# Memory attention in fours of heads: scores in row halves, one score buffer, one group ahead

## The chip, the core and the metric

The kernel runs on one core of one Trainium2 chip. The metric is the time of one execution in microseconds on the device; lower is better. The program is one long kernel with six stages that run one after the other. The change touches the second of them.

## What is computed

The input x has 64 sequences of 128 tokens with 128 features. Six layers are applied, each added to x: causal attention, memory attention, a mixture of experts, an attention with SiLU, an attention over a context, and a feed-forward layer with 4-bit rounding. The stage in question is memory attention (the reference passes it a layer norm of x, and it norms once more by itself):

```python
xn = layernorm(x)                         # over 128 features, x being normed already
q = split_heads(xn @ Wq)                  # 16 heads of 64
k, v = split_heads(xn @ Wkv)
mem = split_heads(memories @ Wm)          # 77 tokens of context
k = concatenate([k, mem]); v = concatenate([v, mem])    # 128 + 77 = 205 keys
attn = softmax(q @ k.T * 64 ** -0.5)
return (attn @ v) @ Wo + bo
```

## The kernel before

Everything is in float32 and x stays in SBUF. `stage_memory_attention` (line 563) writes out by hand, for each engine, the order of its instructions, and joins the engines by semaphores; `over_sequences` (line 75) runs each engine's `step` for the 64 sequences, in pairs of an even and an odd one (p is the parity, which selects the buffer). An engine's queue is in order: an instruction behind a waiting one waits too.

A step has eight groups of two heads (i = 0 to 7). For each group the tensor engine (PE) makes the scores of two heads (`score`, line 671, 128 x 410 in one PSUM bank; two banks `sc` alternate, so scores run two groups ahead). Each head's q stands in a zero-padded 128-row buffer `qx`, so that a matmul over all 128 rows against the two heads' keys gives one head's scores. The vector engine (DVE) takes the minimum of the negated scores (`lowest`, line 755), the scalar engine (ACT) takes exponentials and their sums (`exponentials`, line 895, an activation of 205 columns for each head), DVE divides (`divide`, line 763: a reciprocal and two multiplications), PE transposes (`transposes`, line 685, four 128 x 128 blocks), and the transposed probabilities are copied from PSUM to SBUF (`copy_probs`), by DVE for even i (line 777) and by ACT for odd i (line 906). PE multiplies with the values (`values`, line 697, two heads in column halves of the array).

Between these, in the same queues, stands the work of the next sequence: PE projects q, k, v and the context's values in chunks of 512 columns (`project`, line 645; kinds "q", "k", "v", "mv"), and for every second sequence the context's keys ("mk", four chunks of 308 columns for the pair); ACT copies each chunk out (`copy_projection`, line 863). Two PSUM banks `pj` alternate: chunk k waits until chunk k - 2 is copied (line 649). `CHUNKS` and `SLOT` (lines 615 to 619) say which chunk goes with which group. `project_out` (line 712) makes the output of the sequence before and DVE adds it to x with the bias (`residual`, line 792). Two layer norms stand on DVE (lines 801 to 824), with their reciprocal roots on POOL (`norm_rsqrt`, line 132). The SP queue loads the context for each pair of sequences (line 628).

PE's order in a step, which the change rewrites, is:

```python
for i in range(NP):
    score(b, p, i + 2)          # or of sequence b + 1
    transposes(b, i)
    ...                         # transpose_x, projections of b + 1
    values(b, p, i - 1)         # or of sequence b - 1
    if i == 2 and not first:
        project_out(b - 1)
```

Of the kernel before, what the change touches and what calls it, by code (L numbers as in the profile page):

```python
# [562 lines left out]
def stage_memory_attention(nc, X, w, consts, tiles):  # L563
# [5 lines left out]


    KN = S + CK
    with ExitStack() as ctx:
# [6 lines left out]
        qx = mem.sbuf("qx", [128, 2, XH, 128])  # L579
# [3 lines left out]
        low = mem.sbuf("low", [128, 2, 2])  # L583
        sums = mem.sbuf("sums", [128, 2, 2])
        rec = mem.sbuf("rec", [128, 2, 2])
        pr = mem.sbuf("pr", [128, 2, 2, 256])
        pn = mem.sbuf("pn", [128, 2, 2, 256])
        prT = mem.sbuf("prT", [128, 2, 2, 2, 128])
        oT = mem.sbuf("oT", [128, NP, 128])
# [4 lines left out]
        po = mem.psum("po", [128, 512])  # L594
        pm = mem.psum("pm", [128, 512])
        p_xT, p_y = pm[:, 0:128], pm[:, 128:256]
# [7 lines left out]
        tr_made = mem.sem("tr_made")  # L604
        prT_even, prT_odd = mem.sem("prT_even"), mem.sem("prT_odd")
        pv_made, oT_made = mem.sem("pv_made"), mem.sem("oT_made")
        y_made, y_added, x_written = mem.sem("y_made"), mem.sem("y_added"), mem.sem("x_written")
        ln = NormBuffers(mem, "ln")
        ln2 = NormBuffers(mem, "ln2")

        CHUNKS = [[("mk", 0), ("mk", 1), ("mk", 2), ("mk", 3), ("q", 0), ("k", 0), ("q", 1), ("k", 1), ("v", 0),
                   ("v", 1), ("mv", 0), ("mv", 1)],
                  [("mv", 0), ("mv", 1), ("q", 0), ("k", 0), ("q", 1), ("k", 1), ("v", 0), ("v", 1)]]
        SLOT = [[[0, 1], [2, 3], [4], [5], [6], [7, 8], [9, 10], [11]],
                [[0], [1], [2], [3], [4], [5], [6], [7]]]
# [5 lines left out]
        with nc.Block() as block:  # L625
            @block.sync
            def _(sp):
                def load(j):
                    if due(20 * j - 6):
                        sp.wait_ge(pj_made, 20 * j - 6)  # L630
                    sp.dma_start(cT[:], w["ctxT"].rearrange("(j r) d k -> j d r k", r=2)[j]).then_inc(c_loaded, 16)

                load(0)
                with sp.Fori(1, B // 2) as j:
                    load(j)

            @block.tensor
            def _(pe):
                def transpose_x(b, p):
                    pe.wait_ge(ln2.xn_done, b + 1)  # L640
                    if due(b - 2):
                        pe.wait_ge(y_added, b - 2)
                    pe.transpose(p_xT, ln2.xn[:, p], consts.ident[:]).then_inc(xT_made, 1)

                def project(b, p, k):
# [25 lines left out]
                def score(b, p, i):  # L671
                    n = NP * b + i
                    if due(n - 1):
                        pe.wait_ge(exped, n - 1)
                    if i == 0:
                        pe.wait_ge(ck_moved, b + 1)
                        pe.wait_ge(pj_copied, chunks(b, p) + CHUNKS[p].index(("k", 0)) + 1)
                    if i == 4:
                        pe.wait_ge(pj_copied, chunks(b, p) + CHUNKS[p].index(("k", 1)) + 1)
                    for h in range(2):  # L680
                        last = pe.matmul(sc[:, i % 2, KN * h:KN * h + KN], qx[:, p, 2 * i + h], kT[:, p, i],  # L681
                                         start=True, stop=True)
                    last.then_inc(scored, 1)

                def transposes(b, i):
                    n = NP * b + i
                    pe.wait_ge(normed, 2 * n + 2)
                    if due(NP // 2 * b + i // 2):
                        pe.wait_ge(prT_odd if i % 2 else prT_even, NP // 2 * b + i // 2)
                    for h in range(2):  # L690
                        for t in range(2):
                            o = 256 * h + 128 * t
                            last = pe.transpose(tr[:, i % 2, o:o + 128], pn[:, i % 2, h, 128 * t:128 * t + 128],  # L693
# [3 lines left out]
                def values(b, p, i):  # L697
                    pe.wait_ge(prT_odd if i % 2 else prT_even, NP // 2 * b + i // 2 + 1)
                    if i == 0:
                        pe.wait_ge(pj_copied, chunks(b, p) + len(CHUNKS[p]))  # L700
                    if i % 4 == 0:
                        if due(2 * b + i // 4):
                            pe.wait_ge(oT_made, 2 * b + i // 4)
                    for t, v in enumerate((vt, vm)):
                        for h in range(2):
                            f = XD * (2 * i + h)
                            last = pe.matmul(po[XD * h:XD * h + XD, 128 * (i % 4):128 * (i % 4) + 128],  # L707
                                             v[:, p, f:f + XD], prT[:, i % 2, h, t], start=t == 0, stop=t == 1,
                                             tile_position=(0, XD * h))
                    last.then_inc(pv_made, 1)  # L710

                def project_out(b):
                    pe.wait_ge(oT_made, 2 * b + 2)
                    if due(b):
                        pe.wait_ge(y_added, b)

                    pe.wait_ge(xT_copied, b + 3 if not isinstance(b, int) else min(b + 3, B))
                    for i in range(NP):
                        last = pe.matmul(p_y, oT[:, i], wo[:, i], start=i == 0, stop=i == NP - 1)
                    last.then_inc(y_made, 1)  # L720

                def step(b, p, last):
                    first = isinstance(b, int) and b == 0
                    for i in range(NP):
                        if i < NP - 2:
                            score(b, p, i + 2)
                        elif not last:
                            score(b + 1, 1 - p, i + 2 - NP)
                        transposes(b, i)
                        if i == 0 and not last:  # L730
                            transpose_x(b + 1, 1 - p)
                        if not last:
                            for k in SLOT[1 - p][i]:
                                project(b + 1, 1 - p, k)
                        if i > 0:
                            values(b, p, i - 1)
                        elif not first:
                            values(b - 1, 1 - p, NP - 1)
                        if i == 2 and not first:
                            project_out(b - 1)  # L740
                    if last:
                        values(b, p, NP - 1)
                        project_out(b)

                pe.wait_ge(zeroed, 4)
# [4 lines left out]
                score(0, 0, 1)  # L750
# [3 lines left out]
            def _(dve):  # L754
                def lowest(b, i):
                    n = NP * b + i
                    if due(n - 1):
                        dve.wait_ge(exped, n - 1)
                    dve.wait_ge(scored, n + 1)
                    dve.tensor_reduce(low[:, i % 2], sc[:, i % 2, 0:2 * KN].rearrange("p (h k) -> p h k", h=2),  # L760
                                      AX.X, ALU.min).then_inc(low_found, 1)

                def divide(b, i):

                    n = NP * b + i
                    if due(2 * n - 2):
                        dve.wait_ge(normed, 2 * n - 2)
                    dve.wait_ge(exped, n + 1)
                    dve.reciprocal(rec[:, i % 2], sums[:, i % 2]).then_inc(rec_made, 1)  # L769
                    if due(n - 1):  # L770
                        dve.wait_ge(tr_made, n - 1)
# [1818 lines left out]
```

## Time and profile before

| | before |
|---|---|
| median of 3 runs | 4079.44 us (4078.22 to 4080.56) |
| span of the profiled execution | 4078.1 us |
| that execution's own time, apart from its span | not given; the three runs lie within 2.5 us of the span |
| PE busy over the span | 3652.5 us (90%) |
| DVE, ACT, POOL busy | 63%, 62%, 41% |
| PE clock over the span, mean granted | 0.939 of full |
| first instruction of memory attention | 641.99 us (the first memset) |
| last output projection of the stage, last matmul begins | 2283.3 us |

Times are microseconds from the span's start. A row of a timeline gives the start, the time from start to the last one's end, and the operation; since an engine overlaps neighbouring instructions, the cost of an instruction in its queue is the distance from its start to the next one's start (its slot), which is shorter than its duration. A float32 matmul shows as two records. The bracket at the end is the idle time before, and who ended it. PEclk is the clock that PE was granted, 1.00 being 2.4 GHz and 0.50 being 1.2 GHz.

### The profile page before, as it was taken

Reading aid. Unit: us, or ns where it says so; the run is one execution under the profiler, and the core shown is the slowest. Engines: PE = TensorE matmul, PEld = TensorE weight load, DVE = VectorE, ACT = ScalarE, POOL = GpSimd, SP = SyncE. Lnnn points to the kernel's source line nnn. Section 1 sums busy time; section 2 is a strip of 40 time slices with the busy share of each in tenths; the row PEclk is TensorE's granted clock in tenths of the full one; section 3 lists DMA queues with packets and bytes.
Section 4 is the critical chain, followed back from the end, with each engine's and each line's share of the span. In section 5 each row is a group of like instructions: output and inputs, shape, how many; then the busy total and the mean of one; then the engine's idle time right before and its main releaser. Section 6 shows DMA issues by size and latency. Waiting matters only on the chain. (4 is left out here: it accounts for less than half of the span.)

```text
span 4078.1 us, 99545 instructions
## 1 busy us (share of the span) xinstructions
PE 3652.5 (90%) x26897; PEld 2556.5 (63%) x26989; DVE 2573.4 (63%) x8223; ACT 2526.2 (62%) x9209; POOL 1690.9 (41%) x2468
## 2 busy tenths in 40 slices
PE   8999998999999999999999614879999799995776
PEld 5565666777777777777777513654444466663444
DVE  7888885555555555555555520126666688887997
ACT  6888886666666666666666201235555699993221
POOL 6888882000000000000000142038888577774665
PEclk9999999999999999999999657989999899997776
DMA  4000000000000000000000102210000000000000
GB/s 119 0 0 0 0 0 3 2 2 2 2 2 2 2 2 2 2 2 2 2 2 1 63 26 64 81 44 9 9 9 9 5 6 5 5 5 3 13 10 16
DMA packets 80213, 53.87 MB, mean 13 GB/s; under 512 B 24785, under 2 KB 74397, under 8 KB 80016
## 3 DMA queue, kind: packets, MB, share of 16 engines
q1 hardware_dynamic: 76048, 44.89, 3.9%
q0 software_dynamic: 4096, 8.16, 0.7%
q8 instruction: 31, 0.51, 0.1%
q14 instruction: 38, 0.31, 0.0%
HBM read 32.29 MB, written 20.97 MB: 13 GB/s over the span
## 5 line engine op out<-in xcount | busy, mean ns | idle before, releaser
L135 POOL TENSOR_TENSOR b_ln_var_eps<-b_ln_mean_var,all_eps 128x1 f32<-128x1 f32 x128 | 33.3, 260 | 1476.8 <-DVE b_ln_mean_var L129 1476.8
L681 PE MATMUL b_sc<-b_kT,b_qx 128*128 128x205 f32 x2048 | 485.2, 360 | 1.2 <-ACT b_pr L901 1.2
L901 ACT ACTIVATE b_pr<-b_sc,b_low 128x205 f32<-128x205 f32 x1024 | 431.8, 429 | 68.6 <-DVE b_low L760 64.0
L467 ACT ACTIVATE a_pr<-a_sc,a_low 128x128 f32<-128x128 f32 x1024 | 365.4, 383 | 37.1 <-POOL a_pn L511 26.5
L782 DVE COPY b_prT<-b_tr 128x512 f32<-128x512 f32 x256 | 177.1, 692 | 322.4 <-PE b_tr L693 322.4
L681 PEld LDWEIGHTS b_sc<-b_kT,b_qx 128*128 128x128 f32 x2048 | 330.4, 189 | 78.9 <-issue 77.1
L774 DVE TENSOR_SCALAR b_pn<-b_pr,b_rec 128x205 f32<-128x205 f32 x1024 | 289.4, 325 | 58.8 <-DVE b_rec L769 7.4
L2090 ACT ACTIVATE f_pr<-f_sc,f_low 128x77 f32<-128x77 f32 x1024 | 320.2, 338 | 10.2 <-DVE f_low L1981 2.9
L693 PE MATMUL b_tr<-all_ident,b_pn 128*128 128x128 f32 x2048 | 307.7, 273 | 2.7 <-DVE b_pn L774 2.4
L760 DVE TENSOR_REDUCE b_low<-b_sc 128x2 f32<-128x410 f32 x512 | 295.4, 577 | 19.2 <-PE b_sc L681 19.1
L502 POOL TENSOR_TENSOR a_kx<-a_qk,w_hsel 128x512 f32<-128x512 f32 x256 | 292.1, 1152 | 2.4 <-DVE a_qk L338 2.4
L1488 PE MATMUL d_sc<-d_qx,d_qk 128*128 128x512 f32 x512 | 288.4, 646 | 0.0
L254 PE MATMUL a_sc<-a_kx,a_qk 128*128 128x512 f32 x512 | 262.7, 595 | 11.7 <-POOL a_kx L502 9.2
L769 DVE RECIPROCAL b_rec<-b_sums 128x2 f32<-128x2 f32 x512 | 82.1, 160 | 300.5 <-ACT b_pr L901 300.3
L693 PEld LDWEIGHTS b_tr<-all_ident,b_pn 128*128 128x128 f32 x2048 | 255.1, 140 | 20.8 <-DVE b_pn L774 4.2
L881 ACT ACTIVATE b_qx<-b_pj 64x512 f32<-64x512 f32 x256 | 151.5, 592 | 150.7 <-PE b_pj L658 149.2
L707 PEld LDWEIGHTS b_po<-b_prT,b_vt 128*64 128x64 f32 x2048 | 101.4, 135 | 210.5 <-issue 183.5
L1592 ACT ACTIVATE d_at<-d_sc 128x512 f32<-128x512 f32 x256 | 152.9, 597 | 125.6 <-PE d_po L1498 124.7
L467 ACT ACTIVATION_READ_ACCUMULATOR a_pr<-a_sc,a_low 128x1 f32 x1024 | 227.4, 222 | 0.0
L911 ACT ACTIVATE b_prT<-b_tr 128x512 f32<-128x512 f32 x256 | 153.2, 598 | 119.3 <-PE b_tr L693 119.3
L707 PE MATMUL b_po<-b_prT,b_vt 128*64 128x128 f32 x2048 | 225.4, 298 | 0.0
L2090 ACT ACTIVATION_READ_ACCUMULATOR f_pr<-f_sc,f_low 128x1 f32 x1024 | 223.6, 218 | 0.0
(278 smaller groups left out, 9605.9 us busy)
## 6 DMA issues: line engine op xcount, KB each, us to landing
scratch_x<-r_zeros SPq DMA_DIRECT2D x12, 512.0 KB, 5.0
e_xr<-scratch_x SPq DMA_DIRECT2D x24, 256.0 KB, 3.1
scratch_y<-e_yr SPq DMA_DIRECT2D x24, 256.0 KB, 2.4
all_X<-in_x SPq DMA_DIRECT2D x8, 512.0 KB, 6.8
e_w<-in_e_w SPq DMA_DIRECT2D x16, 256.0 KB, 3.1
out_x<-all_X SPq DMA_DIRECT2D x8, 512.0 KB, 3.2
w_mask<-in_mask SPq DMA_DIRECT2D x1, 2464.0 KB, 10.6
b_cT<-in_ctxT SPq DMA_DIRECT2D x32, 77.0 KB, 1.9
```

Of the source, the lines that this page charges most:

```text
L254: pe.matmul(sc[:, u % 2], qk[:, p, 0], kx[:, p, u], start=False, stop=True).then_inc(scored, 1)
L467: op = act.activation(pr[:, u % 2, g], sc[:, u % 2, 128 * g:128 * g + 128], ACT.Exp, bias=low[:, u % 2, g:g + 1], scale=-1.0, accum_out=su ...
L502: pool.tensor_tensor(kx[:, p, u], qk[:, p, 1].unsqueeze(1).broadcast_to([128, NG, 128]), hsel[:, NG * u:NG * u + NG].unsqueeze(2).broadcas ...
L681: last = pe.matmul(sc[:, i % 2, KN * h:KN * h + KN], qx[:, p, 2 * i + h], kT[:, p, i], start=True, stop=True)
L693: last = pe.transpose(tr[:, i % 2, o:o + 128], pn[:, i % 2, h, 128 * t:128 * t + 128], consts.ident[:])
L707: last = pe.matmul(po[XD * h:XD * h + XD, 128 * (i % 4):128 * (i % 4) + 128], v[:, p, f:f + XD], prT[:, i % 2, h, t], start=t == 0, stop=t ...
L760: dve.tensor_reduce(low[:, i % 2], sc[:, i % 2, 0:2 * KN].rearrange("p (h k) -> p h k", h=2), AX.X, ALU.min).then_inc(low_found, 1)
L774: dve.tensor_scalar(pn[:, i % 2, h, 0:KN], pr[:, i % 2, h, 0:KN], rec[:, i % 2, h:h + 1], None, ALU.mult).then_inc(normed, 1)
L782: dve.tensor_copy(prT[:, i % 2].rearrange("p h t q -> p (h t q)"), tr[:, i % 2])\
L901: op = act.activation(pr[:, i % 2, h, 0:KN], sc[:, i % 2, KN * h:KN * h + KN], ACT.Exp, bias=low[:, i % 2, h:h + 1], scale=-1.0, accum_out ...
L1488: pe.matmul(sc[:, u % 2], qk[:, p, 1], qx[:, p, u], start=True, stop=True).then_inc(scored, 1)
L2090: op = act.activation(pr[:, u % 2, g], sc[:, u % 2, CK * g:CK * g + CK], ACT.Exp, bias=low[:, u % 2, g:g + 1], scale=-1.0, accum_out=sums[ ...
```

## The change

- **Groups.** A step has four groups of four heads (j = 0 to 3), each in two halves (i = 0, 1) of two heads.
- **Scores.** The padded `qx` becomes a dense `q`. A head's scores come from a matmul over 64 rows (`tile_position=(64 * h, 0)`), rows 0 to 63 for h = 0 and 64 to 127 for h = 1, each h into a bank of its own. The two banks now hold one group, so there is one score buffer, and scores run one group ahead. One `lowest` covers four heads (820 columns).
- **Transposed probabilities.** All `copy_probs` are on DVE. `prT` keeps two buffers, now the halves of one group. The values of a group come in one go at the end of the group, for the group itself.
- **Order.** On PE, DVE and ACT it is written anew, see the diff. Chunks go in lists `EARLY` (between the two halves' transposes) and `LATE` (after the second).
- **mv.** The context's values are no longer a matmul of 512 columns but four transposes of the context's keys.
- **PSUM.** `po`, `p_xT` and `p_y` share a bank; `po` holds one group and is copied by four `copy_out` of 256 columns instead of two of 512; `oT` gets two buffers.
- **Norms.** The two layer norms are made in one pass: the second's statistics and application on DVE go, and POOL works out the product of both roots in seven small operations (`both_norms`). The bias is added on POOL (`add_bias`).
- **Start.** The memsets of `qx` and `pr` go. The wait of the context's load is on an earlier chunk, as its buffer is read by mk alone.

The core of the diff (semaphore counts that only follow the new numbering left out):

```diff
-        qx = mem.sbuf("qx", [128, 2, XH, 128])
+        q = mem.sbuf("q", [128, 2, NP, 128])
...
+        EARLY = [[[0, 1, 2, 3], [], [6], [9]], [[], [], [2], [5]]]
+        LATE = [[[4], [5], [7, 8], [10, 11]], [[0], [1], [3, 4], [6, 7]]]
...
-                        half = wm[:].rearrange("p (c i) d -> p c (i d)", c=2)[:, c]
-                        last = pe.matmul(dst[0:CK], cT[:, p], half, start=True, stop=True)
+                        for t in range(4):
+                            last = pe.transpose(dst[0:CK, 128 * t:128 * t + 128], ck[:, 4 * c + t, p], consts.ident[:])
...
+                def score(b, p, j):
+                    n = NJ * b + j
+                    if due(2 * n):
+                        pe.wait_ge(exped, 2 * n)
...
+                    for i in range(2):
+                        for h in range(2):
+                            r = slice(XD * h, XD * h + XD)
+                            last = pe.matmul(sc[:, h, KN * i:KN * i + KN], q[r, p, 2 * j + i],
+                                             kT[r, p, 2 * j + i], start=True, stop=True, tile_position=(XD * h, 0))
                     last.then_inc(scored, 1)
...
+                def values(b, p, j, last_sequence):
+                    n = NJ * b + j
+                    pe.wait_ge(prT_made, 2 * n + 2)
...
             @block.tensor
...
                 def step(b, p, last):
+                    for j in range(NJ):
+                        if j < NJ - 1:
+                            score(b, p, j + 1)
                         elif not last:
+                            score(b + 1, 1 - p, 0)
+                        transposes(b, j, 0)
+                        if j == 0 and not last:
+                            transpose_x(b + 1, 1 - p)
+                        if j == 1 and not first:
+                            project_out(b - 1, 1 - p, NJ * b + 1)
                         if not last:
+                            for k in EARLY[1 - p][j]:
                                 project(b + 1, 1 - p, k)
+                        transposes(b, j, 1)
+                        if not last:
+                            for k in LATE[1 - p][j]:
+                                project(b + 1, 1 - p, k)
+                        values(b, p, j, last)
...
             @block.vector
...
                 def step(b, p, last):
+                    for j in range(NJ):
+                        copy_probs(b, j, 0)
+                        if j == 0 and ahead:
                             norm_statistics(dve, ln, X[:, b + 2], b + 2, p)
...
+                        if more:
+                            lowest(nb, nj)
+                        if j == 0 and ahead:
+                            norm_moments(dve, ln, p)
+                        if more:
+                            divide(nb, nj, 0)
+                        if j == 1 and not (isinstance(b, int) and b == 0):
+                            residual(b - 1)
+                        copy_probs(b, j, 1)
+                        if j == 1 and not last:
+                            move_context_keys(b + 1, 1 - p)
+                        if j == 2 and ahead:
+                            dve.wait_ge(xT_made, b + 1)
                             norm_apply(dve, ln, X[:, b + 2], b + 2, p)
+                        if more:
+                            divide(nb, nj, 1)
...
             @block.scalar
...
                 def step(b, p, last):
+                    for j in range(NJ):
+                        if j > 0:
+                            copy_out(b, p, j - 1)
...
+                        if more:
+                            exponentials(nb, nj, 0)
+                        if j == 0 and not last:
                             copy_xT(b + 1, 1 - p)
+                        if more:
+                            exponentials(nb, nj, 1)
+                            for k in EARLY[1 - p][j]:
                                 copy_projection(b + 1, 1 - p, k)
+                        if not last:
+                            for k in LATE[1 - p][j]:
+                                copy_projection(b + 1, 1 - p, k)
```

(nb, nj) is the next group: (b, j + 1), or (b + 1, 0) after the last of a sequence.

## Rows read from the trace of the kernel before

**Rows 1.** The windows view of the steady part: busy us and instructions by engine, PEclk, DMA

```profile
702.63:2236.00 1533.37, 1533.37 (x11699) 1215.83 (x11697) 866.51 (x2727) 1050.92 (x3093) 98.43 (x242) 1.00 0.01 2
```

**Rows 2.** The instructions of line 719: ns min/median/max, first and last start

```profile
L719 PE MATMUL b_pm<-w_wo,b_oT x1024: 275/275/582, 699.8 to 2283.3; 128*128 128x128 f32 x171
```

**Rows 3.** PE timeline near the stage's end: start us, us, line, operation, count, idle before

```profile
2242.38 2.05 PE L719 MATMUL b_pm<-w_wo,b_oT 128*128 128x128 f32 x16
...
2276.39 0.73 PE L693 MATMUL b_tr<-all_ident,b_pn 128*128 128x128 f32 x4 [1.22 <-DVE b_pn L774]
2277.05 0.70 PE L707 MATMUL b_po<-b_prT,b_vt 128*64 128x128 f32 x4
```

**Rows 4.** PE timeline of one sequence in the steady part, same columns

```profile
1200.83 1.21 PE L662 MATMUL b_pj<-b_cT,w_wm 128*128 128x154 f32 x8
...
1205.37 2.05 PE L719 MATMUL b_pm<-w_wo,b_oT 128*128 128x128 f32 x16
1207.26 0.86 PE L681 MATMUL b_sc<-b_kT,b_qx 128*128 128x205 f32 x4
...
1209.38 0.44 PE L707 MATMUL b_po<-b_prT,b_vt 128*64 128x128 f32 x4
...
1209.97 0.96 PE L681 MATMUL b_sc<-b_kT,b_qx 128*128 128x205 f32 x4
1210.76 0.60 PE L693 MATMUL b_tr<-all_ident,b_pn 128*128 128x128 f32 x4
1211.20 1.06 PE L658 MATMUL b_pj<-b_xT,w_wq 128*128 128x128 f32 x8
1212.19 0.44 PE L707 MATMUL b_po<-b_prT,b_vt 128*64 128x128 f32 x4
```

**Rows 5.** ACT timeline of the same stretch

```profile
1200.21 0.43 ACT L901 ACTIVATE b_pr<-b_sc,b_low 128x205 f32<-128x205 f32 x1
...
1201.09 0.60 ACT L911 ACTIVATE b_prT<-b_tr 128x512 f32<-128x512 f32 x1
1201.59 0.92 ACT L887 ACTIVATE b_ck<-b_pj 128x308 f32<-128x308 f32 x2
...
1224.40 0.46 ACT L860 ACTIVATE b_xT<-b_pm,w_gain 128x128 f32<-128x128 f32 x1 [0.59 <-PE b_pm L643]
```

**Rows 6.** DVE timeline of the same stretch

```profile
1199.87 0.28 DVE L123 BATCH_NORM_STATS2 b_ln_stats<-all_X 128x6 f32 x1
1201.24 0.17 DVE L769 RECIPROCAL b_rec<-b_sums 128x2 f32<-128x2 f32 x1 [1.09 <-ACT b_pr L901]
1201.52 0.57 DVE L774 TENSOR_SCALAR b_pn<-b_pr,b_rec 128x205 f32<-128x205 f32 x2
1202.00 0.58 DVE L760 TENSOR_REDUCE b_low<-b_sc 128x2 f32<-128x410 f32 x1
...
1204.07 0.69 DVE L782 COPY b_prT<-b_tr 128x512 f32<-128x512 f32 x1 [1.40 <-PE b_tr L693]
1204.68 0.15 DVE L769 RECIPROCAL b_rec<-b_sums 128x2 f32<-128x2 f32 x1
...
1208.16 0.58 DVE L760 TENSOR_REDUCE b_low<-b_sc 128x2 f32<-128x410 f32 x1 [0.17 <-PE b_sc L681]
1208.66 0.28 DVE L794 TENSOR_TENSOR all_X<-b_pm,all_X 128x128 f32 x1
```

**Rows 7.** Groups of DVE reductions: count, busy us, mean ns, idle before

```profile
L760 DVE TENSOR_REDUCE b_low<-b_sc 128x2 f32<-128x410 f32 x512 | 295.4, 577 | 19.2 <-PE b_sc L681 19.1
...
L1137 DVE TENSOR_REDUCE r_top<-r_logits 128x64 f32<-128x512 f32 x1 | 0.7, 686 | 0.0
```

**Rows 8.** DVE timeline of the stage's start

```profile
641.99 3.47 DVE L833 MEMSET b_qx<- 128x4096 f32 x1 [2.51 <-PEq L89]
```

**Rows 9.** The windows view of this stage's end and the last stage, as Rows 1

```profile
2270.00:2280.00 10.00, 6.75 (x57) 4.42 (x53) 4.44 (x13) 4.15 (x12) 0.00 (x0) 0.84 0.00 1
...
3800.00:3900.00 100.00, 74.67 (x254) 47.63 (x255) 94.57 (x354) 22.31 (x72) 65.83 (x112) 0.70 0.04 11
```

More of the change, by code:

```diff
@@ L700, in values @@
                         pe.wait_ge(pj_copied, chunks(b, p) + len(CHUNKS[p]))
[L701 to L709, printed above, removed]
@@ L710, in values @@
-                    last.then_inc(pv_made, 1)
[L712 to L717, printed above, removed]
+                        if not last_sequence:
+                            pe.wait_ge(xT_copied, b + 2)
+                    if j == 1 and due(b):
+                        pe.wait_ge(y_added, b)
@@ new lines, in values @@
+                    if due(n):
+                        pe.wait_ge(oT_made, n)
+                    for i in range(2):
+                        for t, v in enumerate((vt, vm)):
+                            for h in range(2):
+                                f = XD * (4 * j + 2 * i + h)
+                                last = pe.matmul(po[XD * h:XD * h + XD, 128 * i:128 * i + 128], v[:, p, f:f + XD],
+                                                 prT[:, i, h, t], start=t == 0, stop=t == 1,
+                                                 tile_position=(0, XD * h))
@@ L718, in project_out @@
+                    last.then_inc(pv_made, 1)
+                def project_out(b, p, free):
+                    pe.wait_ge(oT_made, free)
                     for i in range(NP):
-                        last = pe.matmul(p_y, oT[:, i], wo[:, i], start=i == 0, stop=i == NP - 1)
+                        last = pe.matmul(p_y, oT[:, p, i], wo[:, i], start=i == 0, stop=i == NP - 1)
                     last.then_inc(y_made, 1)
@@ L825, in step @@
-                        if i == 3 and not (isinstance(b, int) and b == 0):
-                            residual(b - 1)
-                        if i == 4 and not last:
-                            move_context_keys(b + 1, 1 - p)
+                        more = j < NJ - 1 or not last
+                        nb, nj = (b, j + 1) if j < NJ - 1 else (b + 1, 0)
+                        if more:
+                            lowest(nb, nj)
+                        if j == 0 and ahead:
+                            norm_moments(dve, ln, p)
@@ L920, in copy_out @@
                                    ACT.Copy).then_inc(oT_made, 1)
                 def step(b, p, last):
[L923 to L934 removed]
+                    for j in range(NJ):
+                        if j > 0:
+                            copy_out(b, p, j - 1)
+                        elif not (isinstance(b, int) and b == 0):
+                            copy_out(b - 1, 1 - p, NJ - 1)
+                        more = j < NJ - 1 or not last
+                        nb, nj = (b, j + 1) if j < NJ - 1 else (b + 1, 0)
+                        if more:
+                            exponentials(nb, nj, 0)
+                        if j == 0 and not last:
```

282 lines of the change are left out of this document (115 added, 167 removed).

## Prediction

> **What bounds the kernel now.** I read the windows view first. Over 1533 us of memory attention PE is busy for 1533.37 us at PEclk 1.00, while DVE is busy for 867 us and ACT for 1051 us [rows 1]: PE alone sets this stage's time. Its period follows from the output projections, one for a sequence: the first begins at 699.8 us for sequence 0 [rows 2], that of sequence 61 at 2242.38 us [rows 3], so a sequence takes 1542.6 / 61 = 25.29 us.
>
> The PE timeline gives the slots, from one start to the next [rows 4]: scores of two heads 0.79 (1209.97 to 1210.76), four transposes 0.44, a chunk of q or k 0.99, the values of two heads 0.59 (1209.38 to 1209.97), the output projection 1.89, and two mk chunks 1.21, so 0.6 each. For v and mv chunks, also 512 columns, I take 0.99. A sequence is 8 x 0.79 + 8 x 0.44 + 4 x 0.99 + 4 x 0.99 + 8 x 0.59 + 1.89 + 1.2 (mk, mean of even and odd) + 0.1 = 25.7, near the 25.29 measured. The slots can be trusted to 2%.
>
> **PE's work after.** If the two row halves run together, the scores of four heads take the slot of two: 4 x 0.79 saved, 3.2 us. The mv chunks become four transposes each: 2 x (0.99 - 0.44) = 1.1 us saved. That leaves 25.3 - 4.3 = 21.0 us a sequence. If PE stayed the bound this would be the new period.
>
> **The loop that the new order closes.** With one score buffer and the values of group n ahead of the scores of group n + 2 on PE, I follow one group from its scores and count what each step waits for:
> - PE: scores of n + 1, slot 0.79, then the transposes of n's first half, 0.60 to their end [rows 4]: 1.39. The scores end earlier (0.96).
> - DVE begins 0.04 after PE's end: scores end at 1207.26 + 0.86 = 1208.12 [rows 4], the reduction begins at 1208.16 [rows 6]. I use 0.04 for every hand-over. The copy of the probabilities stands first in DVE's queue: slot 0.61 (1204.07 to 1204.68) [rows 6]. Total 2.04.
> - The minimum over 820 columns: 577 ns for 410 and 686 ns for 512 make 1.07 ns a column [rows 7], so 0.577 + 410 x 1.07 ns = 1.02, an estimate. 3.06.
> - Hand-over 0.04, then ACT's two exponentials until DVE's reciprocal: 1200.21 [rows 5] to 1201.24 [rows 6], 1.03. 4.13.
> - Reciprocal 0.28, two multiplications 0.48 (1201.24, 1201.52, 1202.00) [rows 6]. 4.89.
> - Only now the copy of the second half, behind the division in DVE's queue: 0.69, and 0.04. 5.62.
> - PE, waiting for it, makes the values of four heads: 2 x 0.59 = 1.18. 6.80. The next scores stand behind them.
>
> So 6.80 us a group or 27.2 a sequence, with no engine full: more than the 25.29 of today. On top:
> - j = 0 has the norm's statistics (0.28 [rows 6]) between the first copy and the minimum, j = 1 the residual (0.28) ahead of the second copy: +0.56.
> - j = 2 and 3 have a third chunk (mv) whose bank comes free by a copy that ACT makes behind both pairs of exponentials: start at 3.10, two pairs at 0.88 (1200.21 to 1201.09 [rows 5]), the copy 0.60, hand-over 0.04, gives 5.50, the transposes 0.44, gives 5.94 against 5.62: +0.32 each, +0.64.
> - j = 0 ahead of an even sequence has four mk chunks between the two transposes, and the third waits for ACT's copy of the first, behind four exponentials and the copy of xT. ACT begins at 3.38, +0.88, xT +0.46, +0.88, copy of a chunk 0.46 (0.92 for two) [rows 5] and 0.04: 6.10; two mk chunks 1.2 [rows 4]: 7.30; transposes 0.60, hand-over, copy 0.69, hand-over: 8.67 against 5.90. +2.77, each second sequence: +1.4.
>
> Together 27.2 + 0.56 + 0.64 + 1.4 = 29.8 us, 4.5 more than today, and 63 periods give +284 us.
>
> **What costs or gives nothing.** ACT loses four copies of probabilities and two of four q copies, DVE gains the four copies and loses a norm's pass: both have room beside a 29 us period [rows 1]. POOL gets seven small operations and the bias; it is busy for 98 of 1533 us [rows 1], and the norm is used two groups later. The four smaller `copy_out` run in ACT's idle time ahead of the minimum. SP's load waits for an earlier chunk, so comes sooner. The output projection (1.89) and the other chunks lie in PE's wait for the second copy (from 1.4 to 5.6 us of a group). If the loop were shorter than 21.0 / 4 = 5.3 us, these would show. At the start the memset of qx goes (3.47 [rows 8]) and one pass of the norm: about 5 us less.
>
> Sum without the clock: 4078 + 284 - 5 = 4357 us, by the profiled span of 4078.1; the median is 1.3 us above it, too little to carry.
>
> **The row halves.** No row shows them. The nearest is column halves: four value matmuls of 128 columns take 0.59, four full ones of a q chunk 0.99 [rows 4], so two halves do overlap, if not wholly. Bounds for a group's scores: 0.4 (half the slot that I take; four heads without any weight-load time between) and 1.58 (no overlap). I take 0.79, two full slots of one head each. The Trainium skill's "TensorEngine Tiling (Array Packing)", section Tiling Modes, says that tiles work independently, which would give 0.79 as well, but also that changing the tiling mode drains the engine, which speaks against this change, as scores now are a mode of their own. The rows bound that: values to scores, a column mode and then a full one, take 0.59, and wholly overlapped halves without a drain would take 0.99 / 2 = 0.50, so a switch costs at most 0.09. Two more switches in a group would make the sum 0.18 x 4 x 64 = 46 us longer; I leave this to the range.
>
> **The clock.** PE now idles. In the first group of a sequence it has nothing from 1.8 us (both transposes) until q, which needs xT at 4.76. The trace shows what such gaps do: at the stage's end, with waits of 1.22 us, the transposes stretch from 0.60 to 0.73 and the values from 0.44 to 0.70 [rows 3], and the granted clock is 0.84 [rows 9], part of it at 1.2 GHz. At 1.2 GHz the loop's PE parts, 0.79 + 0.44 + 1.18, grow by 2.4 us. Bounds: nothing, or one such group in each sequence, 2.4 x 64 = 154 us. I take the middle, +77. Forecast 4357 + 77 = 4434.
>
> **Rivals.**
> - *Row halves in turn.* Scores 1.58 at the head of the loop: +0.79 x 4 x 64 = +202, 4640 us. For it: no row. Against: the column halves. Here the change would not do what it says.
> - *Low clock throughout.* The last stage, PE busy 75%, is granted 0.70 [rows 9], more than half of its time at 1.2 GHz. At 0.75, half the time, each group loses 1.2 us: +5 us a sequence on 4357, about 4670. Against: PE here works 21.0 of 29.8 us in bursts of full speed. The skill's "TensorE: Matmul & The Clock Gate", section "Why this matters for your kernels", names idle gaps between bursts as what takes the clock down; by it this rival gains.
> - *Short scores.* 0.4 instead of 0.79 and no clock loss: 4357 - 100 = 4257.
> - *PE stays the bound, faster.* Should the second copy not wait for the division, that is, should the loop of a group be under 5.3 us, the period is 21.0: 4078 - 4.3 x 63 - 5 = 3802. It turns faster than today already when the loop falls under (25.29 - 2.6) / 4 = 5.7 us. The place is DVE's queue between minimum and second copy. Against: the order is written out, and 1.03 + 0.28 + 0.48 are measured; the sum would need to be 1.1 us wrong.
>
> **How the numbers follow.** Forecast case 0.62, own range 4357 to 4520; row halves in turn 0.15; low clock throughout 0.10; short scores 0.08; PE-bound or a loop under 5.7, 0.03; within 0.2% of today 0.02 (0.2%, 8 us, is what a measurement of this kernel can tell). The range 4290 to 4650 holds the forecast, the row halves in turn and half of the short scores; most of the low clock and the faster case are left out. Faster 0.03, same 0.02, slower 0.95. The likeliest case gives 4434.
>
> **What would show it.** The PE timeline should have gaps ended by DVE's copy (`b_prT`) ahead of the values, in every group; PE busy near 75% in this stage; a distance of about 6.8 us from scores to scores, 7 for j = 0 and near 9.6 ahead of even sequences; the reduction at 1.0 us; PEclk under 1.00 around j = 0. Wrong it would be if PE were busy throughout, if scores of four heads took 1.6 us, or if DVE's second copy began before the division ended.

## The result and the profile after

The changed kernel takes 4523.88 us in the median of 4 runs (4522.9 to 4524.87), the kernel before 4080.0 beside it. The ratio is 1.1096, with a 95% interval of 1.1078 to 1.1114: 444 us slower. Forecast were 4434 us, 354 more than before, in a range of 4290 to 4650.

The page of the changed kernel, its part 1:

```profile
PE 3588.0 (79%) x27245; PEld 2537.5 (56%) x27245; DVE 2645.3 (59%) x7965; ACT 2304.2 (51%) x8953; POOL 1766.3 (39%) x2724
```

PE's share falls from 90% to 79% of the span. The windows view of the stage says more; the row answers to [rows 1] (PE, PEld, DVE, ACT, POOL busy, then PEclk, DMA, GB/s):

```profile
900.00:2100.00 1200.00, 889.23 (x7306) 727.13 (x7305) 581.11 (x1521) 513.62 (x1738) 96.93 (x296) 0.92 0.01 1
```

PE, busy for the whole of its stretch before, is now busy for 889 of 1200 us, and its clock is 0.92 instead of 1.00. DVE and ACT are busy for less than half. No engine is full: the stage is bound by a chain. The starts of the output projection, one for a sequence, give the period (PE timeline, start, us, line, operation, count):

```profile
2525.30 1.95 PE L721 MATMUL b_pm<-w_wo,b_oT 128*128 128x128 f32 x16
...
2555.54 1.95 PE L721 MATMUL b_pm<-w_wo,b_oT 128*128 128x128 f32 x16
...
2590.16 1.95 PE L721 MATMUL b_pm<-w_wo,b_oT 128*128 128x128 f32 x16
```

One sequence takes 30.24 us and the next 34.62, as every second one brings the four mk chunks: 32.43 in the mean against 25.29 before, and 63 x 7.14 = 450 us. The stage's first scores begin at 659.73 us instead of 666.76, and its last output projection at 2736.3 instead of 2283.3 (begin of its last matmul): 453 us later.

The program as a whole is only 443 us longer (spans of 4521.1 and 4078.1), since 10 us come back behind the stage. The attention with SiLU, whose code the change does not touch, lasts 462.9 us instead of 475.7, from its first matmul to its last, and 462.8 to 463.0 in the traces of all nine kernels that have the change. One vector operation of its norm (`d_ln_xn` from `d_z`) takes 561 ns in the mean of 64, where it took 878; why is not shown. The last stage lasts 360.4 instead of 355.0, and varies from 350.7 to 360.4 among the nine kernels.

The PE timeline of one sequence shows its groups, from scores to scores (brackets: idle time before, and who ended it):

```profile
1226.91 0.97 PE L682 MATMUL b_sc<-b_kT,b_q 64*128 64x205 f32 x8
1227.80 0.66 PE L694 MATMUL b_tr<-all_ident,b_pn 128*128 128x128 f32 x4
...
1230.52 1.06 PE L655 MATMUL b_pj<-b_xT,w_wk 128*128 128x128 f32 x8
1232.86 0.44 PE L713 MATMUL b_pm<-b_prT,b_vt 128*64 128x128 f32 x4 [1.29 <-DVE b_prT L785]
...
1233.89 0.97 PE L682 MATMUL b_sc<-b_kT,b_q 64*128 64x205 f32 x8
...
1239.49 0.66 PE L667 MATMUL b_pj<-all_ident,b_ck 128*77 128x128 f32 x4 [1.83 <-ACT b_q L865]
...
1248.33 0.97 PE L682 MATMUL b_sc<-b_kT,b_q 64*128 64x205 f32 x8
...
1253.53 2.05 PE L655 MATMUL b_pj<-b_xT,w_wq 128*128 128x128 f32 x8 [3.09 <-ACT b_xT L846]
1255.50 0.70 PE L713 MATMUL b_pm<-b_prT,b_vt 128*64 128x128 f32 x4
...
1257.12 0.97 PE L682 MATMUL b_sc<-b_kT,b_q 64*128 64x205 f32 x8
```

The first group shown lasts 6.98 us (1226.91 to 1233.89). PE has made scores, transposes, the output projection and a chunk by 1231.58, and stands 1.29 us until DVE's copy lets the values start. The next two last 14.44 us together (1233.89 to 1248.33), 7.22 each; here the mv transposes wait 1.83 us for ACT's copy of a q chunk. The fourth, the first of its sequence, lasts 8.79: PE waits 3.09 us for xT, and then the q chunk takes 2.05 us instead of 1.06, and the first values 0.70 instead of 0.44: PE runs at 1.2 GHz here (granted clock 0.81 from 1248.3 to 1257.1). The same place ahead of an even sequence:

```profile
1215.29 0.97 PE L682 MATMUL b_sc<-b_kT,b_q 64*128 64x205 f32 x8
...
1216.79 1.21 PE L659 MATMUL b_pj<-b_cT,w_wm 128*128 128x154 f32 x8
1221.71 1.57 PE L659 MATMUL b_pj<-b_cT,w_wm 128*128 128x154 f32 x8 [3.70 <-ACT b_ck L871]
...
1223.92 1.92 PE L655 MATMUL b_pj<-b_xT,w_wq 128*128 128x128 f32 x8
```

Two mk chunks take 1.21 us, the other two wait 3.70 us for a copy by ACT, and the q chunk that follows takes 1.92 us instead of 1.06: 11.62 us from scores to scores.

In the sequence whose first group is this one of 8.79 us, the low clock returns in the third and fourth groups, which take 8.0 us each instead of 7.22:

```profile
1264.10 0.97 PE L682 MATMUL b_sc<-b_kT,b_q 64*128 64x205 f32 x8
...
1269.71 0.66 PE L667 MATMUL b_pj<-all_ident,b_ck 128*77 128x128 f32 x4 [1.83 <-ACT b_q L865]
...
1272.14 1.74 PE L682 MATMUL b_sc<-b_kT,b_q 64*128 64x205 f32 x8
```

The four-head scores take 1.74 us instead of 0.97, behind a wait of 1.83 us. The wait of the same length at 1239.49 is followed by scores of 0.97, so its length alone does not decide.

What PE waits for over the 1200 us (waits view: us in total, times, longest):

```profile
PE b_pj L667 <- ACT b_vt L874: 70.0, 37, 1.9
PE b_pj L667 <- ACT b_q L865: 67.6, 37, 1.8
PE b_pj L659 <- ACT b_ck L871: 66.7, 18, 3.7
PE b_pj L655 <- ACT b_xT L846: 58.8, 19, 3.1
PE b_pm L713 <- DVE b_prT L785: 47.7, 37, 1.3
```

Of these 311 us only 47.7 are ended by DVE's copy of the probabilities, in one group of four. The other 263 are ended by copies that ACT makes behind exponentials.

DVE and ACT in the group that begins at 1226.91 (same columns):

```profile
1228.57 0.69 DVE L785 COPY b_prT<-b_tr 128x512 f32<-128x512 f32 x1 [2.89 <-PE b_tr L694]
1229.18 1.00 DVE L761 TENSOR_REDUCE b_low<-b_sc 128x4 f32<-128x820 f32 x1
1231.18 0.17 DVE L770 RECIPROCAL b_rec<-b_sums 128x2 f32<-128x2 f32 x1 [1.00 <-ACT b_pr L886]
...
1231.93 0.28 DVE L797 TENSOR_TENSOR all_X<-b_pm,all_X 128x128 f32 x1
```

```profile
1230.21 0.43 ACT L886 ACTIVATE b_pr<-b_sc,b_low 128x205 f32<-128x205 f32 x1 [2.74 <-DVE b_low L761]
```

Copy, minimum over 820 columns (1.00 us), exponentials from 1230.21, reciprocal at 1231.18, then the multiplications: the order and the durations of the sum. The residual follows at 1231.93, then the second copy, and the values at 1232.86.

### The profile page after: what moved, and what is told of

The parts are those of the page before. It is cut to its first block and busy times, and to the rows that moved or that the text cites. A ratio compares the mean times of both kernels' runs of the same rounds, so it can differ in the third digit from the quotient of the medians.

```text
span 4521.1 us, 99164 instructions
## 1 busy us (share of the span) xinstructions
PE 3588.0 (79%) x27245; PEld 2537.5 (56%) x27245; DVE 2645.3 (59%) x7965; ACT 2304.2 (51%) x8953; POOL 1766.3 (39%) x2724
## 5 line engine op out<-in xcount | busy, mean ns | idle before, releaser
L785 DVE COPY b_prT<-b_tr 128x512 f32<-128x512 f32 x512 | 351.9, 688 | 747.1 <-PE b_tr L694 747.1
L713 PE MATMUL b_pm<-b_prT,b_vt 128*64 128x128 f32 x2048 | 244.5, 323 | 93.7 <-DVE b_prT L785 93.6
L682 PE MATMUL b_sc<-b_kT,b_q 64*128 64x205 f32 x2048 | 274.1, 390 | 2.9 <-ACT b_pr L886 2.9
L761 DVE TENSOR_REDUCE b_low<-b_sc 128x4 f32<-128x820 f32 x256 | 257.1, 1004 | 24.5 <-DVE b_ln_stats L123 17.6
L667 PE MATMUL b_pj<-all_ident,b_ck 128*77 128x128 f32 x512 | 84.8, 288 | 234.7 <-ACT b_vt L874 119.4
L655 PE MATMUL b_pj<-b_xT,w_wq 128*128 128x128 f32 x1024 | 192.4, 350 | 97.8 <-ACT b_xT L846 97.8
L655 PEld LDWEIGHTS b_pj<-b_xT,w_wq 128*128 128x128 f32 x1024 | 176.1, 259 | 104.7 <-issue 104.7
L713 PE MATMUL b_pm<-b_prT,b_vm 128*64 128x128 f32 x2048 | 224.5, 302 | 0.0
L667 PEld LDWEIGHTS b_pj<-all_ident,b_ck 128*77 128x77 f32 x512 | 55.2, 147 | 299.5 <-ACT b_vt L874 172.2
L895 ACT ACTIVATE b_oT<-b_pm 128x256 f32<-128x256 f32 x256 | 98.1, 383 | 243.2 <-PE b_pm L713 243.2
```

Source lines behind the costliest of these rows:

```text
L655: last = pe.matmul(dst[:, 128 * t:128 * t + 128], src[:, 4 * c + t], xT[:], start=True, stop=True)
L682: last = pe.matmul(sc[:, h, KN * i:KN * i + KN], q[r, p, 2 * j + i], kT[r, p, 2 * j + i], start=True, stop=True, tile_position=(XD * h, 0))
L713: last = pe.matmul(po[XD * h:XD * h + XD, 128 * i:128 * i + 128], v[:, p, f:f + XD], prT[:, i, h, t], start=t == 0, stop=t == 1, tile_posi ...
L785: dve.tensor_copy(prT[:, i].rearrange("p h t q -> p (h t q)"), tr[:, i]).then_inc(prT_made, 1)
```

## The experiments

All kernels start from the kernel after the change. They ran in three batches, each on one chip with runs of the kernel before among them: e, b, f and a (before: 4081.0 us in the median), d and c (4081.5), c2 and c3 (4075.7). Times are medians; between batches the ratios compare better than the times.

| experiment | us | ratio to before, 95% interval |
|---|---|---|
| the change itself | 4523.9 | 1.1078 to 1.1114 |
| e: gaps of PE filled | 4389.7 | 1.0744 to 1.0782 |
| d: scores over full rows | 4825.1 | 1.1806 to 1.1855 |
| b: ACT copies first chunks ahead | 4311.3 | 1.0550 to 1.0587 |
| f: mk chunks behind the transposes | 4517.8 | 1.1058 to 1.1098 |
| a: f, and DVE's second copy ahead of the minimum | 5055.9 | 1.2376 to 1.2423 |
| c: b and a, with the transposes ahead of all chunks | 4081.4 | 0.9990 to 1.0016 |
| c2: c, a third mk chunk copied ahead | 3980.0 | 0.9752 to 0.9786 |
| c3: c2 and one filling matmul | 3988.5 | 0.9773 to 0.9807 |

### e: how much is the clock?

```diff
+                def fill(n):
+                    for _ in range(n):
+                        pe.matmul(spare[:], wq[:, 0], wv[:, 0], start=True, stop=True)
...
                             for k in EARLY[1 - p][j]:
+                                if p == 1 and k == 2 and j == 0:
+                                    fill(3)
                                 project(b + 1, 1 - p, k)
                         transposes(b, j, 1)
                         if not last:
-                            for k in LATE[1 - p][j]:
+                            if p == 0 and j == 0:
+                                fill(3)
+                            for n, k in enumerate(LATE[1 - p][j]):
+                                if n == 1:
+                                    fill(1)
                                 project(b + 1, 1 - p, k)
```

`spare` is a PSUM bank that nothing reads. In group 1 the list LATE has one entry, so nothing is filled there.

> The changed kernel with extra float32 matmuls of 512 columns into an unused PSUM bank, results unused, where PE waits: three in the first group of a sequence, one ahead of each mv chunk (0.86 us each at the full clock). Theory, that the idle gaps let PE's clock fall and this costs 2.2 us a sequence: PEclk rises from 0.92 to near 1.00 in the stage and 139 us go, 4385, though PE has more to do. Rival, that the groups of 8.8 and 11.6 us are long because of waits on other engines and not by the clock: no gain, 4524 or slower by the extra work, up to 4 us a sequence.

Measured: 4389.7 us, 134 less than the change although PE has some five matmuls more in each sequence. The windows view and the PE timeline of one sequence:

```profile
900.00:2100.00 1200.00, 1032.78 (x8208) 763.38 (x8209) 620.38 (x1625) 551.01 (x1862) 104.90 (x320) 1.00 0.01 1
```

```profile
1499.94 0.97 PE L683 MATMUL b_sc<-b_kT,b_q 64*128 64x205 f32 x8
...
1507.16 0.97 PE L683 MATMUL b_sc<-b_kT,b_q 64*128 64x205 f32 x8
...
1514.38 0.97 PE L683 MATMUL b_sc<-b_kT,b_q 64*128 64x205 f32 x8
...
1521.81 0.97 PE L683 MATMUL b_sc<-b_kT,b_q 64*128 64x205 f32 x8
...
1528.79 0.97 PE L683 MATMUL b_sc<-b_kT,b_q 64*128 64x205 f32 x8
```

PEclk is 1.00. The groups last 7.22, 7.22, 7.43 and 6.98 us (1499.94 to 1528.79): 28.85 for the sequence, 7.43 where it had been 8.79. The groups of 8.0 us are gone too. The expectation was 4385 us. So the clock had cost 134 us, 2.1 us a sequence, and what is left is the loop at the full clock. The extra matmuls fit into the waits: 3 x 0.86 us where PE stood for 3.09 and 3.70, one where it stood for 1.83.

### d: do the row halves overlap, and does it matter?

```diff
-        q = mem.sbuf("q", [128, 2, NP, 128])
+        qx = mem.sbuf("qx", [128, 2, XH, 128])
...
-                            last = pe.matmul(sc[:, h, KN * i:KN * i + KN], q[r, p, 2 * j + i],
-                                             kT[r, p, 2 * j + i], start=True, stop=True, tile_position=(XD * h, 0))
+                            last = pe.matmul(sc[:, h, KN * i:KN * i + KN], qx[:, p, 4 * j + 2 * i + h],
+                                             kT[:, p, 2 * j + i], start=True, stop=True)
```

With it the memset of `qx` and the two half-height copies of each q chunk come back.

> The changed kernel with only the scores undone: the padded q buffer again, each head's scores a matmul over all 128 rows, so four heads in turn. Theory, scores stand at the head of the closed loop and the row halves do run together: the slot grows from 0.90 to 1.6 us and the loop with it, 0.70 x 4 x 64 = 179 us on 4524, 4703, less what the busier PE keeps of its clock, so 4640 to 4703. Rival, that the score time is hidden beside DVE and ACT: 4524 within 20 us. Rival, that row halves bring nothing: 4524 too, but with the scores' slot equal in both kernels.

Measured: 4825.1 us, 301 more. The PE timeline:

```profile
1501.06 1.66 PE L681 MATMUL b_sc<-b_kT,b_qx 128*128 128x205 f32 x8
1502.55 0.60 PE L693 MATMUL b_tr<-all_ident,b_pn 128*128 128x128 f32 x4
...
1507.79 0.67 PE L667 MATMUL b_pj<-all_ident,b_ck 128*77 128x128 f32 x4 [2.41 <-ACT b_qx L867]
```

The slot of four heads is 1.49 us (1501.06 to 1502.55) against 0.89 in row halves (1226.91 to 1227.80 above): the halves do overlap. The size was missed by 120 us. Two things go that way, and I have not told them apart. ACT copies a q chunk in two pieces of 0.6 us, and the mv transposes wait behind them (2.41 us here), which I had left out; and the clock falls to 0.87 in this stage instead of rising, as I had thought. The rival that scores are hidden is refuted, and with it the doubt whether row halves bring anything.

### b: the waits for chunk copies

```diff
+        FIRST = [[[0, 1], [], [6], [9]], [[], [], [2], [5]]]
...
+                        if j == 0 and not last:
+                            copy_xT(b + 1, 1 - p)
+                        if not last:
+                            for k in FIRST[1 - p][j]:
+                                copy_projection(b + 1, 1 - p, k)
                         if more:
                             exponentials(nb, nj, 0)
-                        if j == 0 and not last:
-                            copy_xT(b + 1, 1 - p)
-                        if more:
                             exponentials(nb, nj, 1)
```

The other chunks are copied behind the exponentials, as before.

> Only ACT's order changes: the copy of xT and the first chunks (mk 0 and 1, the third chunk of q and k, the first of v) are copied ahead of both pairs of exponentials, in the time in which ACT waits for the minimum. Theory: PE's waits for chunk copies (q0, mk 2, mv) go, the long gaps with them, and each group falls to the bare loop, 6.91 us with the scores at the measured 0.90: 4 x 6.91 + 0.56 = 28.2 us a sequence instead of 32.43, 266 us less, 4258, PEclk near 1.00, and the values wait for DVE's copy in every group. Rival, that these waits are hidden beside DVE's copy: within 20 us of 4524. Rival, that the exponentials are delayed by the copies ahead of them: slower than 4524.

Measured: 4311.3 us, 213 less than the change. PE timeline:

```profile
1524.19 0.97 PE L683 MATMUL b_sc<-b_kT,b_q 64*128 64x205 f32 x8
...
1527.80 0.60 PE L668 MATMUL b_pj<-all_ident,b_ck 128*77 128x128 f32 x4
1529.95 0.44 PE L714 MATMUL b_pm<-b_prT,b_vt 128*64 128x128 f32 x4 [1.54 <-DVE b_prT L786]
...
1530.97 0.97 PE L683 MATMUL b_sc<-b_kT,b_q 64*128 64x205 f32 x8
...
1544.16 0.70 PE L714 MATMUL b_pm<-b_prT,b_vt 128*64 128x128 f32 x4 [2.98 <-DVE b_prT L786]
```

As expected, the mv transposes no longer wait (1527.80), the values wait for DVE's copy, and a group lasts 6.78 us (1524.19 to 1530.97), a little under the bare loop of 6.91. Of the 266 us expected 213 came. What the expectation missed: where q no longer waits for xT, the idle time moves behind it, 2.98 us ahead of the values (1544.16), and the clock still falls there. PEclk over 1200 us is 0.96.

### f and a: the copy ahead of the minimum

f moves the four mk chunks behind the second half's transposes (`EARLY` and `LATE` of the first group). a adds:

```diff
                         copy_probs(b, j, 0)
+                        copy_probs(b, j, 1)
                         if j == 0 and ahead:
                             norm_statistics(dve, ln, X[:, b + 2], b + 2, p)
...
-                        copy_probs(b, j, 1)
```

> The four mk chunks move behind the second half's transposes (from the early list to the late list); nothing else. Theory, a closed loop in which the first group ahead of an even sequence is held by the chunks that wait for ACT: the transposes (0.85 us there, at the low clock) leave the stretch between the mk chunks and the values, 0.85 x 32 = 27 us less than the changed kernel's 4523.9, so 4497, and the group takes 10.8 instead of 11.6 us. Rival, that the group is held by DVE's copy of the second half: that copy then comes 3 us sooner and about 90 us go, 4430.

> As f_mk_late, and DVE makes the copy of the second half ahead of the minimum instead of behind the division. Rival, the plain reading of the loop as I summed it (the copy waits for the division, 3.5 us into the group, and nothing else binds): the values start 2.8 us after the scores and each group shortens by 1.1 us, 280 us less than f_mk_late, about 4215. Theory, that ACT's copies of chunks behind the exponentials bind just behind it, and that on PE the second half's transposes stand behind an early chunk or the output projection: the minimum, the exponentials and the chunk copies come 0.6 us later in group 0, and up to 1.5 us later in groups 1 to 3, so it is slower than f_mk_late by some 100 to 260 us, 4600 to 4760.

f measured 4517.8 us, 6 less than the change. The rival, 90 less, falls: DVE's copy did not hold that group. But the 27 us did not come either. The group lasts 11.30 instead of 11.62 us (scores at 1535.69 and 1546.99 in its PE timeline), and other groups lengthen by as much: from the first output projection to the last it is 2026.0 us in f and 2027.2 in the change. The low clock only meets other groups (0.91 over the 1200 us against 0.92). Of the 6 us 3 come ahead of the first output projection and 2 behind the stage.

a measured 5055.9 us, 538 more than f. The plain reading of my own loop, that only the copy's place binds, would have given 280 less. One group on PE and DVE:

```profile
1511.34 1.74 PE L682 MATMUL b_sc<-b_kT,b_q 64*128 64x205 f32 x8
...
1513.87 1.02 PE L662 MATMUL b_pj<-w_wv,b_xT 128*128 128x512 f32 x2
1514.73 0.60 PE L694 MATMUL b_tr<-all_ident,b_pn 128*128 128x128 f32 x4
...
1519.39 0.66 PE L667 MATMUL b_pj<-all_ident,b_ck 128*77 128x128 f32 x4 [3.19 <-ACT b_vt L874]
...
1521.29 1.74 PE L682 MATMUL b_sc<-b_kT,b_q 64*128 64x205 f32 x8
```

```profile
1515.44 0.69 DVE L785 COPY b_prT<-b_tr 128x512 f32<-128x512 f32 x1 [0.60 <-PE b_tr L694]
1516.05 1.00 DVE L761 TENSOR_REDUCE b_low<-b_sc 128x4 f32<-128x820 f32 x1
```

```profile
1517.08 0.43 ACT L886 ACTIVATE b_pr<-b_sc,b_low 128x205 f32<-128x205 f32 x1 [5.25 <-DVE b_low L761]
```

Now everything is in one line: the second half's transposes stand behind the v chunk (1514.73), DVE's second copy behind these (1515.44), the minimum behind the copy (1516.05), the exponentials at 1517.08, ACT's copy of the chunk behind the exponentials, and the mv transposes wait 3.19 us for it, then the values. 9.95 us a group (1511.34 to 1521.29), with the clock at 0.83 over the stage. I had the sign and the places, not the size. The low clock, at which scores take 1.74 us, was not in that sum; how much of the miss is its share was not measured.

### c, c2 and c3: the loop opened

c takes a and b together and moves the transposes out of the chunks' way:

```diff
-        EARLY = [[[0, 1, 2, 3], [], [6], [9]], [[], [], [2], [5]]]
-        LATE = [[[4], [5], [7, 8], [10, 11]], [[0], [1], [3, 4], [6, 7]]]
+        EARLY = [[[], [], [], []], [[], [], [], []]]
+        LATE = [[[0, 1, 2, 3, 4], [5], [6, 7, 8], [9, 10, 11]], [[0], [1], [2, 3, 4], [5, 6, 7]]]
+        FIRST = [[[0, 1], [], [6], [9]], [[], [], [2], [5]]]
...
+                        transposes(b, j, 1)
                         if j == 1 and not first:
                             project_out(b - 1, 1 - p, NJ * b + 1)
...
                         copy_probs(b, j, 0)
+                        copy_probs(b, j, 1)
...
+                        if j == 1 and not (isinstance(b, int) and b == 0):
+                            residual(b - 1)
                         if more:
                             divide(nb, nj, 0)
```

> The changed kernel with the orders of three engines altered together: DVE copies both halves ahead of the minimum (and adds the residual ahead of the division); PE makes the second half's transposes directly behind the first's, ahead of all chunks and of the output projection; ACT copies xT and the first chunk(s) ahead of the exponentials, as in b_act_first. Theory: the reordering of DVE cost time in a_copy_before_min only because the transposes and the chunk copies stood behind other work. With these moved, the loop is scores 0.90, transposes 0.66, two copies 1.22, minimum 1.00, four exponentials 1.84 and hand-overs, 5.7 us, and the values hide in it: 4 x 5.7 + 0.9 + 0.3 = 24.0 us a sequence, 4521 - 8.4 x 63 = 3990, under the kernel before. Rival, that DVE's copy ahead of the minimum is bad in itself, as a_copy_before_min suggests: slower than b_act_first's 4311.

Measured: 4081.4 us, the same as before within the interval of 0.9990 to 1.0016, and 230 less than b. So DVE's order that cost 538 us in a does no harm where the transposes and the chunk copies are out of its way: the rival falls. How the 230 us divide between DVE's order and PE's is open, as b with PE's new order alone was not run. The same total hides a stage that is longer still: its last output projection begins at 2298.2 us, 15 later than before, and the shorter attention with SiLU gives 13 back. The PE timeline:

```profile
1501.36 0.97 PE L683 MATMUL b_sc<-b_kT,b_q 64*128 64x205 f32 x8 [0.46 <-ACT b_pr L884]
...
1507.08 0.97 PE L683 MATMUL b_sc<-b_kT,b_q 64*128 64x205 f32 x8 [0.49 <-ACT b_pr L884]
...
1513.63 1.16 PE L656 MATMUL b_pj<-b_xT,w_wq 128*128 128x128 f32 x8 [2.10 <-ACT b_ck L869]
...
1515.75 0.97 PE L683 MATMUL b_sc<-b_kT,b_q 64*128 64x205 f32 x8
```

A group is 5.72 us (1501.36 to 1507.08), as summed, and what ends it are the exponentials, no longer the values. The 91 us that are missing stand mainly in the first group ahead of an even sequence, where q waits 2.10 us for the third mk chunk's copy. The group shown lasts 8.67 us (1507.08 to 1515.75) and is one of the shortest: where the clock falls behind that wait it lasts up to 10.27, and the mean is 9.59. c2 makes that copy earlier:

```diff
-        FIRST = [[[0, 1], [], [6], [9]], [[], [], [2], [5]]]
+        FIRST = [[[0, 1, 2], [], [6], [9]], [[], [], [2], [5]]]
```

c3 adds one filling matmul (`fill(1)` of e) behind the chunks of each sequence's first group.

> c_loop_opened with one entry more: ACT copies mk chunk 2 ahead of the exponentials too, in a gap of 0.8 us that it has there. Theory: the 2.1 us for which q of the next sequence waits in the first group ahead of even sequences go, with part of the low clock that follows that gap: 8.67 to about 6.7 us in that group, 2.0 x 32 = 63 us under the 4081 of c_loop_opened, 4018, 1.5% under the kernel before. Rival, that the exponentials come later by the copy and the scores, which wait for them, take the gain back: 4070 to 4090.

> c2_third_mk_first with one extra float32 matmul of 512 columns (0.86 us, result unused) into an unused PSUM bank ahead of the values of each sequence's first group, where PE then waits 1.8 us for the exponentials. Theory: the rest of the low clock goes, PEclk near 1.00 instead of 0.96, and the period falls to the 23.6 us of groups at the full clock: 3970 to 4000. Rival, that the clock costs nothing where the loop runs over ACT and DVE: the same time as c2_third_mk_first within 10 us, or more by the extra work.

Measured: c2 3980.0 us, ratio 0.9752 to 0.9786, 2.3% under the kernel before, and 101 under c (95 by the ratios) instead of the 63 expected. I had summed from the short group: in the trace of c2 that group lasts 6.56 us every time, 3.03 under the mean of c, or 97 us over 32 groups, wait and low clock together. In the stage alone c2 gains 91 us on the kernel before (last output projection at 2192.5 us instead of 2283.3). c3 3988.5 us. The windows view of c2 and of c3:

```profile
900.00:2100.00 1200.00, 1100.71 (x9879) 901.84 (x9874) 792.59 (x2059) 677.72 (x2358) 130.64 (x400) 0.98 0.01 2
```

```profile
900.00:2100.00 1200.00, 1123.07 (x9966) 893.76 (x9962) 789.21 (x2052) 676.47 (x2355) 130.07 (x400) 1.00 0.01 2
```

c2 has a clock of 0.98 by itself; c3 brings it to 1.00 and is 8.5 us slower (in the traces its last output projection begins 9.2 us later, at 2201.7). Ahead of even sequences, where PE had no gap left, the matmul lengthens the first group from 6.56 to 7.42 us; the second groups of every other sequence, 6.33 us in the mean of c2 with the low clock in some, are 5.71 in c3. The time lies in the range that I expected, but for the rival's reason: the extra work costs more than the clock gives back. So c2 is the version to keep: it has the row halves and the single score buffer of the change and beats both kernels.

## Why the prediction was right, and where its terms were off

**PE bound before: right.** PE's work after was put at 21.0 us a sequence and never became the bound. The rival of 3802 us falls.

**The closed loop: right, and sized within 2%, but what ends it was foreseen in part.** At the full clock (e) a group is 6.98 us with the residual (7.08 summed) and 7.22 with the third chunk (7.12 summed). The first group is 7.43, and 10.23 with mk (7.08 and 9.85 summed), so a sequence is 30.25 in the mean of both kinds against 29.8. The extras of mv and mk are in the trace where the sum put them, in the waits of 1.83 and 3.70 us. The minimum over 820 columns took 1.00 us against 1.02. One sign that I named did not come: waits ended by DVE's copy in every group. They stand in one group of four; in the others copies by ACT end later. For mv I had summed this; in the first group ahead of an odd sequence I had taken DVE's second copy as the last, and there it is xT (3.09 us) and the q chunk behind it, and f shows that with mk it is not DVE's copy either. The loop as I summed it, 6.80 us and ended by DVE's copy, appears when ACT's copies are out of the way: 6.78 in b, where scores that take 0.10 us more than I put are made up for by the other terms. That it is a loop, not a sum of loads, is shown by b, c and c2, in which no operation goes and only orders change: 4523.9 to 4311.3, 4081.4 and 3980.0 us.

**The scores: the mechanism right, 0.10 us too small.** Row halves overlap, 0.89 us for four heads instead of the 0.79 taken; 1.49 in turn (d). Four groups, 64 sequences, 0.10 us: 26 us. The rival of 1.58 falls. The Trainium skill's "TensorEngine Tiling (Array Packing)", section Tiling Modes, has both sides, tiles that work independently and a drain at a change of mode. The rows agree with the first; the 0.10 us may be the second, but no run here takes the drain apart.

**The clock: the term that was mis-sized.** I took the middle of 0 and 154 us, +77, which was a guess between bounds and not a reading. Filling the gaps gave 134 us back (e). I had counted one first group in each sequence, and for these the middle was about right: 8.79 against 7.43 us, and 11.62 against 10.23. What I had not counted is that the clock falls again in other groups, the two of 8.0 us against 7.22 in every second sequence. By rows it falls behind PE's waits of 3.09 and 3.70 us, behind some of 1.83, and it stays up when they are filled. The Trainium skill's "TensorE: Matmul & The Clock Gate", section "Why this matters for your kernels", names idle gaps between bursts of matmuls as what takes the clock down, and the trace agrees: 3.09 us of waiting, then 2.05 us for a chunk of 1.06. The advice there is about longer gaps than the 1.83 us behind which the clock also fell here, so for those the measurement decides.

**The miss as a whole.** By the spans it is 87 us (4521.1 against 4434). The stage itself ends 97 us later than my sum has it: 57 by the clock, 26 by the scores, and 14 that I cannot divide. The 10 us that the stages behind it gave back were not in the prediction at all, and that they make the miss smaller is luck.

**The start: the first scores come 7 us earlier, where I had put 5.**

The rival of a low clock throughout (4670) has not come: 0.92, not 0.75.

## What to carry to other kernels

Before moving work off the busiest engine, follow one round of the new order from an instruction to the same instruction of the next round, through every queue. If that round is longer than the busy engine's load, the saving is lost and more; here some 4.3 us a sequence saved on PE (my sum) came with 7.1 us more a sequence. With a single buffer, put what ends the round (the minimum, the exponentials) behind as little as possible in every queue at once: moving one item in one queue alone cost 538 us, and together with what stands ahead of it and with ACT's copies it brought the kernel back from 4518 to 4081. And count the clock where PE begins to wait: filling the gaps gave 134 us back.

## What the runs showed that I had not expected

Matmuls whose results nobody reads made the kernel 134 us faster (e), where PE waited anyway, and 8.5 us slower once the gaps were small (c3). The order change of a cost 538 us; my upper bound was 260. The clock of the stage stood at 0.92 in the change, 0.87 in d and 0.83 in a, lower the longer the groups were. And a stage that the change does not touch became 13 us shorter.
